# Dividing the values' outputs instead of the softmax probabilities, by reciprocals repeated over partitions

## The reference

```python
q = _rmsnorm(x @ Wq); k = _rmsnorm(x @ Wk); v = x @ Wv       # (B, T, 16, 64)
gate = softplus(einsum('bthd,hd->bht', k, u_n) / sqrt(D))
bias = -dist * omega_eff * gate                               # causal: -inf above the diagonal
scores = einsum('bihd,bjhd->bhij', q, k) * scale + bias
attn = softmax(scores, axis=-1)
y = einsum('bhij,bjhd->bihd', attn, v).reshape(B, T, H * D)
return y @ Wproj
```

## Time and profile before

| | us |
|---|---|
| median of 3 runs | 1352.42 |
| lowest and highest | 1348.07, 1359.08 |
| span of the profiled execution | 1353.4 |
| PE busy | 1309.2 |
| DVE busy | 1090.3 |
| ACT busy | 947.7 |

### The profile page before, as it was taken

How to read it: one execution, slowest core, us unless ns; L and a number is a source line. 1 busy time by engine, 2 the same in 40 slices (tenths; PEclk the granted TensorE clock), 3 DMA queues, 4 the chain that set the end, 5 groups by cost and what they waited for, 6 DMA issues and landing times. The chain is left out here.

```text
span 1353.4 us, 32125 instructions
## 1 busy us (share of the span) xinstructions
PE 1309.2 (97%) x11499; PEld 1103.9 (82%) x11499; DVE 1090.3 (81%) x3337; ACT 947.7 (70%) x2376; POOL 190.3 (14%) x564
## 2 busy tenths in 40 slices
PE   5899999999999999999999999999999799999999
PEld 3688888887978888797888878888888588888888
DVE  6869996999699789969996998799699867777663
ACT  6759885888588678858885887688598724444333
POOL 4512111111011111101111111111111100000000
PEclk8889999999999999999999999999999999999999
DMA  6452231332323222322322233233232322111100
GB/s 216 171 173 88 73 132 59 110 116 74 102 74 131 80 89 87 104 88 88 119 93 92 84 102 109 67 108 103 77 99 72 108 82 62 55 56 55 55 17 32
DMA packets 90831, 125.17 MB, mean 92 GB/s; under 512 B 8761, under 2 KB 77105, under 8 KB 90673
## 3 DMA queue, kind: packets, MB, share of 16 engines
q1 hardware_dynamic: 90352, 123.11, 28.2%
q10 hardware_dynamic: 320, 0.00, 0.0%
HBM read 103.69 MB, written 19.40 MB: 91 GB/s over the span
## 5 line engine op out<-in xcount | busy, mean ns | idle before, releaser
L1192 ACT ACTIVATE prob<-prob,low 128x512 f32<-128x512 f32 (+3 forms) x512 | 280.8, 551 | 115.7 <-DVE low L1348 115.7
L1348 DVE CUSTOM_DVE_ANT_0 prob<-at,mask 128x512 f32<-128x512 f32 (+3 forms) x512 | 219.6, 485 | 10.3 <-PE at L939 10.3
L926 PE MATMUL at<-w_hi,c_lo 128*128 128x386 f32 x512 | 190.1, 371 | 1.5 <-DVE area_raw L1293 1.5
L926 PE MATMUL at<-w_hi,c_hi 128*128 128x386 f32 x512 | 174.3, 340 | 0.0
L926 PE MATMUL at<-w_lo,c_hi 128*128 128x386 f32 x512 | 174.0, 340 | 0.0
L1361 DVE TENSOR_SCALAR prob<-prob,rec 128x512 f32<-128x512 f32 (+3 forms) x512 | 169.3, 394 | 4.5
L978 PE MATMUL at<-ident,prob 128*128 128x128 f32 x1280 | 164.3, 275 | 3.2 <-DVE low L1348 1.8
L1006 PE MATMUL at<-probT,v 128*32 128x512 f32 (+3 forms) x2048 | 152.6, 438 | 3.8 <-DVE probT L1371 2.6
L978 PEld LDWEIGHTS at<-ident,prob 128*128 128x128 f32 x1280 | 142.4, 140 | 10.6 <-DVE yT_lo L1377 1.6
L1006 PEld LDWEIGHTS at<-probT,v 128*32 128x32 f32 x2048 | 67.3, 110 | 89.8 <-issue 80.7
L1201 ACT ACTIVATE probT<-at 128x512 f32<-128x512 f32 (+1 forms) x256 | 130.3, 536 | 4.4 <-PE at L978 1.5
(11 more groups left out here) (254 smaller groups left out, 3195.9 us busy)
## 6 DMA issues: line engine op xcount, KB each, us to landing
area_w<-in_L_ffn_w SPq DMA_DIRECT2D x65, 1024.0 KB, 5.5
bias<-in_L_ffn_w SPq DMA_DIRECT2D x160, 32.0 KB, 4.4
x_in<-in_L_attn_x SPq DMA_DIRECT2D x8, 512.0 KB, 5.5
xr<-in_L_attn_x SPq DMA_DIRECT2D x8, 512.0 KB, 4.6
eo_d<-hidT SPq DMA_DIRECT2D x32, 128.0 KB, 1.8
x_d<-xr SPq DMA_DIRECT2D x8, 512.0 KB, 2.9
area_raw<-x_d SPq DMA_DIRECT2D x8, 512.0 KB, 3.9
out<-area_raw SPq DMA_DIRECT2D x7, 512.0 KB, 3.1
```

Source lines behind the costliest of these rows:

```text
L926: m = eng.matmul(bQ[n % 2][:, 0:W], a[:, (j // HP) % 2, k, n * P:(n + 1) * P], w[:, k, j % HP, :], start=start, stop=(k == KC - 1 and a is ...
L1192: eng.activation(sl, sl, ACT.Exp, scale=-1.0, bias=low[:, i:i + 1], accum_out=den[:, i:i + 1]).then_inc(exp_done.sem, 1)
L1348: eng.tensor_tensor_reduce(out=prob[s % 2][h][:, off[c]:off[c + 1]], in0=bC[i][:, at:at + (c + 1) * P], in1=mask[:, (NT - 1 - c) * P:T], s ...
```

## The change

The probabilities stay undivided. At the end of turn s DVE takes all 8 columns of reciprocals at once (`invert`). SP stores them to a scratch tensor rec_d in HBM in the order (head, query), 1024 single elements, waits until that is complete, waits until head 0's probabilities have been transposed, and loads each head's row of 512 reciprocals back, repeated over that head's 64 partitions (`spread_rec`). They land in the first 512 columns of prob[s % 2][0], which nobody reads any more (`share_of`). In turn s + 1 DVE multiplies the values' output in bY by them (`scale_y`), in place in that tile; ACT's `copy_y` and DVE's `low_y` (before: `copy_y`) then read the tile instead of PSUM. y_done counts twice a turn, and PE's scores wait only for the first of the two. PE's transposes wait for the exponentials instead of p_done.

```diff
+    rec_d = scratch("rec_d", (2, 2, T))
...
-        rec_done, p_done, pt0_D, pt1_D = ev("rec_done", 2), ev("p_done", 2), ev("pt0_D", 1), ev("pt1_D", 1)
+        rec_done, pt0_D, pt1_D = ev("rec_done", 1), ev("pt0_D", 1), ev("pt1_D", 1)
+        rec_store, rec_load = ev("rec_store", 1, 16), ev("rec_load", 2, 16)
...
-        y_done = ev("y_done", 1)
+        y_done = ev("y_done", 2)
...
+        def share_of(s):
+
+            return prob[s % 2][0][:, 0:T]
...
+                def spread_rec(s):
+                    eng.wait_ge(rec_done.sem, rec_done.at(s))
+                    with nc.allow_non_contiguous_dma(reason="1024 reciprocals, one to a query and head"):
+                        eng.dma_start(rec_d[s % 2].rearrange("h (c p) -> p (h c)", p=P), rec[:, :]).then_inc(rec_store.sem, 16)
+                    eng.wait_ge(rec_store.sem, rec_store.at(s))
+                    eng.wait_ge(pe_p0.sem, pe_p0.at(s))
+                    for h in range(2):
+                        eng.dma_start(share_of(s)[h * D:(h + 1) * D, :], rec_d[s % 2, h, :].partition_broadcast(D)).then_inc(rec_load.sem, 16)
...
                 for s in range(NTURN + 1):
                     b = s // HP
+                    if s > 0:
+                        spread_rec(s - 1)
...
-                    eng.wait_ge(y_done.sem, y_done.at(s - 2))
+                    eng.wait_ge(y_done.sem, y_done.at(s - 2, 1))
...
-                    eng.wait_ge(p_done.sem, p_done.at(s, 1))
+                    eng.wait_ge(exp_done.sem, exp_done.at(s, 7))
...
-                    eng.wait_ge(p_done.sem, p_done.at(s, 2))
+                    eng.wait_ge(exp_done.sem, exp_done.at(s))
...
-                                       accum_out=den[:, i:i + 1]).then_inc(exp_done.sem, 1)
+                                       accum_out=den[:, NT * h + c:NT * h + c + 1]).then_inc(exp_done.sem, 1)
...
-                    eng.wait_ge(pe_y.sem, pe_y.at(s))
-                    eng.activation(yT_hi[:, s % HP, :], bY[:, :], ACT.Copy).then_inc(y_hi_done.sem, 1)
+                    eng.wait_ge(y_done.sem, y_done.at(s, 1))
+                    eng.activation(yT_hi[:, s % HP, :], share_of(s), ACT.Copy).then_inc(y_hi_done.sem, 1)
...
-                def divide(s, half):
...
+                def invert(s):
+                    eng.wait_ge(exp_done.sem, exp_done.at(s))
+                    eng.wait_ge(rec_store.sem, rec_store.at(s - 1))
+                    eng.reciprocal(rec[:, :], den[:, :]).then_inc(rec_done.sem, 1)
...
-                def copy_y(s):
+                def scale_y(s):
+                    eng.wait_ge(rec_load.sem, rec_load.at(s))
+                    eng.wait_ge(pe_y.sem, pe_y.at(s))
+                    eng.tensor_tensor(share_of(s), bY[:, :], share_of(s), ALU.mult).then_inc(y_done.sem, 1)
+
+                def low_y(s):
...
-                    if s < NTURN:
-                        divide(s, 0)
+                    prepare(s, 2)
+                    if s > 0:
+                        scale_y(s - 1)
                     if begins_in(s) is not None:
                         add_bias(begins_in(s))
-                    prepare(s, 2)
...
-                        copy_y(s - 1)
+                        low_y(s - 1)
...
-                        divide(s, 1)
+                        invert(s)
```

More of the change, by code:

```diff
@@ L99, in build @@
         half = sb("half", [P, 16])
-        carrier = whole.enter_context(nc.semaphore("carrier"))
         with ExitStack() as ctx, nc.Block() as block:
@@ L114, in build @@
         g = dict(nc=nc, B=B, T=T, C=C, NT=NT, KC=KC, H=H, D=D, HP=HP, E=E, F=F, NB=NB, HC=HC, M1=M1, TOPK=TOPK, GRP=GRP,
-                 sb_in=sb_in, banks=banks, ident=ident, merged=merged, half=half, carrier=carrier,
-                 xnT_hi_d=xnT_hi_d, xnT_lo_d=xnT_lo_d, pick_d=pick_d, x1_d=x1_d, eo_d=eo_d)
+                 sb_in=sb_in, banks=banks, ident=ident, merged=merged, half=half,
+                 xnT_hi_d=xnT_hi_d, xnT_lo_d=xnT_lo_d, pick_d=pick_d, x1_d=x1_d, eo_d=eo_d, rec_d=rec_d)
         g.update(second_layer_inputs(nc, g, whole))
@@ L677, in attend @@
         "B", "T", "C", "NT", "KC", "H", "D", "HP", "E", "F", "GRP"))
-    merged, eo_d = g["merged"], g["eo_d"]
+    merged, eo_d, rec_d = g["merged"], g["eo_d"], g["rec_d"]
     FW = F // GRP
@@ L1351, in lows @@
                             accum_out=low[:, k:k + 1]).then_inc(maxed.sem, 1)
-                def divide(s, half):
-                    eng.wait_ge(exp_done.sem, exp_done.at(s, 4 * half + 4))
-                    eng.reciprocal(rec[:, 4 * half:4 * half + 4], den[:, 4 * half:4 * half + 4]).then_inc(rec_done.sem, 1)
-                    eng.wait_ge(rec_done.sem, rec_done.at(s, half + 1))
-                    for h in range(2):
-                        for c in ((3, 1), (2, 0))[half]:
-                            k = order.index((c, h))
-                            sl = prob[s % 2][h][:, off[c]:off[c + 1]]
-                            p = eng.tensor_scalar(sl, sl, rec[:, k:k + 1], None, ALU.mult)
-                        if half == 1:
-                            p.then_inc(p_done.sem, 1)
+                def invert(s):
+                    eng.wait_ge(exp_done.sem, exp_done.at(s))
+                    eng.wait_ge(rec_store.sem, rec_store.at(s - 1))
+                    eng.reciprocal(rec[:, :], den[:, :]).then_inc(rec_done.sem, 1)
                 def copy_p(s, h):
@@ L1376, in copy_y @@
                     eng.wait_ge(y_hi_done.sem, y_hi_done.at(s))
-                    eng.tensor_tensor(yT_lo[:, s % HP, :], bY[:, :], yT_hi[:, s % HP, :].bitcast(F32), ALU.subtract).then_inc(y_done.sem, 1)
+                    eng.tensor_tensor(yT_lo[:, s % HP, :], share_of(s), yT_hi[:, s % HP, :].bitcast(F32), ALU.subtract).then_inc(y_done.sem, 1)
                 def add_bias(m):
```

## The result

The changed kernel takes 1659.84 us (median of 4 runs, 1647.82 to 1665.30), the kernel before 1353.83 (4 runs): ratio 1.225, 95% interval 1.220 to 1.229. It is slower by 306 us, and the prediction (1352, range 1344 to 1368) is wrong. What happened is the first rival, the late reciprocals, to which the prediction gave a chance of 0.14, far beyond the 1414 at which it was priced. The profiled execution has a span of 1663.6 us.

A forecast was written before the change was run, and what follows sets the result against it. PE, busy 97% of the span, was taken to bound the kernel; +0.5 us (GELU turns) and -1.0 (last pass) gave -0.5 on the profiled 1353.4 us, and from the median some 1352 us, range 1344 to 1368.

The forecast's parts named there:

- the late reciprocals: Rival, chance 0.14: store and loads land late, DVE, ACT and PE wait; 62 us at both upper ends, 1414.
- the store's price: Store of 1024 single reciprocals on SP: taken as 4.5 us from issue to landing, with 5.7 as upper end.
- the threshold: Reciprocals come late if the store takes over some 7 us, or store and loads together over 9.9 us.
- The prediction's own sum: Reciprocals' way through memory: 5 + 0.1 + 0.5 + 3.2 lands at +8.8 us, 2.0 us ahead; cost 0.
- the cover of 10.8 and the slack of 0.27: Values end 10.8 us after a turn's first scores; 0.27 us more are left before PE notices.
- The division was waited for nearly nowhere: Attention turns: removing the division's 169.3 us of DVE gains 0 in steady turns, because PE fills them.
- The added link: DVE's multiplication between values and yT_hi: fits into ACT's 0.83 us of idle time, 0 to 0.2 us a turn.
- the link does not fit: Rival, chance 0.10: handoffs or SBUF reads take 0.2 us more, 5 to 14 us in 48 turns, 1357 to 1366.
- GELU turns: Turns with s % 4 == 2, where ACT is late: only its slower copy counts, 15 x 0.036 = 0.5 us.
- The loads: Two loads repeating the reciprocals' rows: 3.2 us to landing taken, their own queue being empty by then.
- The last pass: Turn 63 and the pass after: first add of expert outputs 1.0 us earlier, bounds -4 and +3.
- DVE's time is worth something: Rival, chance 0.05: earlier minima and exponentials gain 11 us in GELU turns, the last pass 4.0: 1337.

The follow-up runs named there:

- e4_read: Changed kernel with the store replaced by a load of 1024 single biases, and the repeated rows taken from weights: 1347.74 us.
- e13: Control: changed kernel's store of 1024 adjacent single elements, with the two loads taking rows of the weights: 1620.6 us.
- e11: Changed kernel with the 1024 single elements stored 32 bytes apart instead of 4, loads from the weights: 1347.65 us.
- e1_rows: Changed kernel with reciprocals stored as 128 rows of 32 bytes instead of 1024 single elements: 1349.26 us against 1349.61, ratio 0.998.
- e7_own64: Changed kernel with 1024 single elements 8 bytes apart, a partition's eight together in 64 bytes, loads from the weights: 1401.09 us.
- e12_step8: Changed kernel with 1024 single elements in its own order, 8 bytes apart, loads from the weights: 1359.85 us.
- e8_blocks: Changed kernel, correct results: DVE transposes reciprocals in 32 by 32 blocks, four transfers store 128-byte rows: 1353.08 us against 1353.82, ratio 0.998.
- e9_dve_hi: e8_blocks with yT_hi made by DVE instead of ACT in the 16 GELU turns: 1344.27 us against 1355.15, ratio 0.992.

## Why the prediction was wrong

**The failed step is the store's price.** It reads: "So they are nearer to the lower end ... A store queued behind it lands at +5, that is 4.5 us after its issue". Measured: 10.75 us. The conclusion came from the 1024 single biases, and of those it was right: "the single elements can have added little over 0.5 us" fits the 3.7 us of e4_read. But they are a read. Both bounds missed the operation: the lower (eo_d) was a store of long rows, the upper (5.7, the biases) a read, so the upper end bounded nothing, and the range built on it could not hold the time. What it would have needed is a row of single elements written next to each other, and it said itself that no row showed such a write; the honest upper end was open.

**Why it is dear.** Shown: neighbouring 4-byte elements, written singly, cost 6.0 us more (e13 against e11) than the same number of packets of the same size 32 bytes apart, and nearly all of that comes below 16 bytes. The Trainium skill ("DMA: Bandwidth & Descriptors", "Rules for kernel authors") has one descriptor per element for such a store, and the packets agree: 167629 against 110286 in e1_rows, 57343 more, for 64 stores of 1024 pieces instead of 128 (57344). The same page ("Specifications") puts a read-modify-write on transfers below 512 bytes. The size alone is not what these runs show: rows of 32 bytes (3.65 us) and single elements 32 bytes apart (4.19 us) are far below 512 and cost little. Shown too: the time lies behind the packets. In the changed kernel they are over 3.4 us after the store's issue (3.0 in e11_step32), and then 7.4 us pass until the loads' issue (1.1 in e11_step32); and with 128 adjacent elements the 16 steps of completion come one by one. A read-modify-write of a small piece of memory, for which the next writer of that piece has to wait, would give this picture; that is argued and not shown. It stays open why e7_own64 is slower than e12_step8, and why the steps of 128 adjacent elements are as much as 0.36 us apart.

**The rival's mechanism was right, its size was not.** The order in which engines would stand (DVE with yT_lo, qT_lo and kT_lo behind the multiplication, ACT with qT_hi and kT_hi, PE at the scores) is that of the waits above, and the threshold held (e12 and e7). The price was 1.3 us x 48; it is 299 / 63 = 4.7 us a turn, GELU turns included. The prediction's own sum was sound: with the measured 10.75 for the store and 3.6 for the loads it gives a landing at 0.5 + 10.75 + 0.6 + 3.6 = +15.5 us, 4.4 us beyond the cover of 10.8 and the slack of 0.27. Turn 28, whose store took 11.60 us and was issued 0.5 us later than reckoned (as it was in the median turn), has it at +16.6 (689.69 - 673.12).

**Steps that held**, seen in e1_rows and e8_blocks, where the store is quick:
- The division was waited for nearly nowhere: without it the ratio is 0.998. DVE's 967.6 us and PE's 1307.2 in e1_rows are those forecast (965, and within 2 of 1309).
- The added link fits into ACT's idle time: qT_hi without a wait, the median of the turns with s % 4 below 2 is 13.93 us in e1_rows and was 14.01, no cost. The rival "the link does not fit" did not come about.
- GELU turns: +0.5 us in all was forecast, for 15 turns; there are 16. The medians, 14.55 against 14.52, bear it out; the sum of the 16 is 1.9 us longer, which the other turns make up for.
- The loads: 2.8 us to landing in e1_rows, 3.2 taken.
- The last pass: -1.0 us was forecast, within -4 and +3. In e1_rows PE's first product of the expert outputs stands 22.5 us behind the first scores of turn 63, before 24.9: 2.3 us earlier.
- DVE's time is worth something: not by itself (e8_blocks), so that rival fell too. But 11 us of its 15 were reckoned in the right place: e9_dve_hi gets 9.3 us in all, out of those turns (6.4) and the ones behind them (3.1), once an instruction is moved from ACT to DVE. ACT's fixed order was the lock, as said.

## What to carry to other kernels

Before a small tensor is turned round through memory, look at which side is written element by element, and at what lies between neighbours there: let each engine write runs (transpose on chip first, or let the reader gather), or keep single elements 16 to 32 bytes apart. Price a write by a row of a write with the same stride; where there is none, the upper end is open, and it should be tried alone before a chain is hung on it. Freed time on an engine that nobody waits for is worth nothing until something from the late engine's chain is moved into it.

## What the runs showed of the hardware

- Writing 1024 single 4-byte elements from SBUF to memory: 10.75 us adjacent, 5.77 us 8 bytes apart, 4.62 us 16 bytes, 4.19 us 32 bytes, 4.15 us 64 bytes. Reading 1024 adjacent ones: 3.7 us.
- 128 adjacent single elements (512 bytes) took 8.28 us, 128 rows of 32 bytes (4 KB) at most 3.65 us.
- The time of the adjacent store lies behind its packets: in turn 28 issued at 674.13, the DMA engines moved nothing from 677 to 685, and the loads were issued at 685.73. The 16 steps of completion of 128 adjacent elements came one by one from 2.9 to 8.3 us, spaced ones from 2.6 to 3.5.
- DVE's 128x512 copy from SBUF to SBUF took 0.43 us in the turn shown (0.515 in the mean of 16), the one from PSUM 0.68, while ACT's is the slower from SBUF (0.628 against 0.593).
- After 3.4 us of idle time PE's granted clock fell to its lower level 1.9 us after the work had come back (turn 29, 694.2), for 3.4 us. In turn 28, after 4.0 us of idle time, it fell 0.6 us after, so the delay is not fixed.
